# Four blocks on Trainium2: the turned row maxima of the first attention move to an edge tile's bank and three chunks later, and thirteen instead of eleven matmuls sum the NF4 planes

## What is computed

```python
# first attention, for each of the 16 batches (mask = layer norm of x, 128 x 512)
x = jnp.transpose(mask, (0, 2, 1))                  # 512 rows of 128
q, k, v = jnp.split(x @ w_in.T + b_in, 3, axis=-1)  # 8 heads of 16
scores = jnp.einsum('bqhd,bkhd->bhqk', q, k) / jnp.sqrt(d)
scores = jnp.where(jnp.abs(idx[:, None] - idx[None, :]) <= 64, scores, neg)
attn = jax.nn.softmax(scores, axis=-1)              # subtracts each row's maximum
o = jnp.einsum('bhqk,bkhd->bqhd', attn, v).reshape(n, t, e) @ w_out.T + b_out
out = jnp.einsum('nit,io->not', jax.nn.relu(transpose(o)) * encodings, w_ct) + b_ct
# NF4 round trip of the three feed-forward weights (1408 x 512 each)
idx = jnp.argmin(jnp.abs(scaled[:, None] - NF4), axis=-1)   # 16 levels
w = NF4[idx] * block_scale                                  # a scale for each 64 weights
```

## Time and profile before

| what | value |
| --- | --- |
| device time, median of 3 runs (lowest, highest) | 1466.54 us (1466.11 to 1466.81) |
| span of the profiled execution | 1463.7 us |
| TensorE matmul busy, share of that span | 1354.5 us, 93% |
| TensorE weight load busy | 813.1 us, 56% |
| VectorE busy | 1002.8 us, 69% |
| ScalarE busy | 791.5 us, 54% |
| GpSimd busy | 249.2 us, 17% |
| first attention, loop of batches | 44 to 490 us |
| of it the steady batches 2 to 13 | 119 to 433 us |

### The profile page before, as it was taken

How to read it: one execution, slowest core, us unless ns; L and a number is a source line. 1 busy time by engine, 2 the same in 40 slices (tenths; PEclk the granted TensorE clock), 3 DMA queues, 4 the chain that set the end, 5 groups by cost and what they waited for, 6 DMA issues and landing times. The chain is left out here.

```text
span 1463.7 us, 28639 instructions
## 1 busy us (share of the span) xinstructions
PE 1354.5 (93%) x8666; PEld 813.1 (56%) x8666; DVE 1002.8 (69%) x3234; ACT 791.5 (54%) x1802; POOL 249.2 (17%) x265
## 2 busy tenths in 40 slices
PE   3678999999999799999989999999789999999998
PEld 1345555555555444444455555555434777777774
DVE  8889999999997646456546788887659654545211
ACT  4777888888888733332357677776530233332331
POOL 4100000000000100000010000002411255555552
PEclk7699999999999999999999999999999999999999
DMA  8534344343440300000020000000322588888885
GB/s 261 145 87 99 91 107 106 86 119 90 107 104 17 145 1 0 0 0 0 0 75 15 16 16 14 14 1 2 146 85 93 184 247 251 255 257 246 255 233 115
DMA packets 63186, 149.52 MB, mean 102 GB/s; under 512 B 10792, under 2 KB 27830, under 8 KB 58892
## 3 DMA queue, kind: packets, MB, share of 16 engines
q1 hardware_dynamic: 49836, 115.70, 26.1%
q0 software_dynamic: 13280, 32.93, 9.6%
HBM read 113.21 MB, written 35.39 MB: 102 GB/s over the span
## 5 line engine op out<-in xcount | busy, mean ns | idle before, releaser
L776 DVE CUSTOM_DVE_ANT_0 masked_scores<-ps_max,band_mask 128x192 bf16<-128x192 f32 (+1 forms) x512 | 177.2, 383 | 20.5 <-PE ps_max L505 13.9
L383 ACT ACTIVATE probs_t<-ps_sc 128x448 f32<-128x448 f32 x256 | 138.7, 542 | 80.4 <-PE ps_sc L525 78.1
L1255 PE MATMUL f_ps<-f_xt,w_t 128*128 (+1 forms) x704 | 160.2, 382 | 2.5 <-ACT w_t L1310 2.5
L377 ACT ACTIVATE nf_above<-nf_scaled,nf_sign_at 128x512 f16<-128x512 bf16 x231 | 161.5, 715 | 0.0
L2803 DVE TENSOR_TENSOR d_inter<-d_silu_g,d_su 128x384 f32<-128x384 f32 x32 | 17.7, 554 | 159.6 <-PE d_su L2487 154.4
L1927 ACT ACTIVATE c_probs<-d_sg,c_negmax 128x128 f32<-128x128 f32 x256 | 90.3, 365 | 58.1 <-DVE c_negmax L2012 57.7
L1255 PEld LDWEIGHTS f_ps<-f_xt,w_t 128*128 128x128 bf16 x704 | 69.3, 98 | 86.7 <-issue 5.0
L2320 POOL DMA_INDIRECT out<-d_h,d_scatter_now x64 | 97.2, 1519 | 108.3 <-DMA out<-d_h,d_scatter_now 92.9
L505 PE MATMUL ps_max<-k_stack,q_stack 96*128 96x192 bf16 (+1 forms) x512 | 96.5, 272 | 19.8 <-DVE row_max L776 13.8
L2671 DVE TENSOR_SCALAR d_onehot<-d_slot_no,d_pos 128x192 bf16<-128x192 bf16 x512 | 101.0, 288 | 0.3 <-PE d_lb L2388 0.3
L505 PEld LDWEIGHTS ps_max<-k_stack,q_stack 96*128 96x128 bf16 x512 | 46.2, 101 | 92.1 <-issue 46.9
(11 more groups left out here) (381 smaller groups left out, 2830.1 us busy)
## 6 DMA issues: line engine op xcount, KB each, us to landing
d_wgu<-in_ex_gu SPq DMA_DIRECT2D x32, 1024.0 KB
d_wdown<-in_ex_d SPq DMA_DIRECT2D x32, 512.0 KB
dr_parts<-qk_parts SPq DMA_DIRECT2D x32, 384.0 KB, 4.8
q_stack<-dr_parts SPq DMA_DIRECT2D x32, 192.0 KB, 2.7
k_stack<-dr_parts SPq DMA_DIRECT2D x32, 192.0 KB, 3.3
out<-x_sb SPq DMA_DIRECT2D x21, 256.0 KB, 2.2
nf_w<-in_nf_w POOLq DMA_DIRECT2D x3, 1408.0 KB, 10.2
q_stack<-dr_parts SPq DMA_DIRECT2D x32, 128.0 KB, 2.4
```

The source lines that it names most:

```text
L377: act.activation(above[:, g, k, :], lvl[:, g, :], ACT.Sign, bias=cut[:, k - NDV:k - NDV + 1]).then_inc(s_sg, 1)
L383: act.activation(pt[:, c, :], SP[c % 2][:].rearrange("p a w -> p (a w)")[:, a:z], ACT.Exp, scale=D0 ** -0.5).then_inc(s_e, 1)
L776: op = dve.tensor_tensor_reduce(masked[:, c % 2, k, off:off + hi - lo], M[c % 2][:, k, off:off + hi - lo], mask[:, k, off:off + hi - lo], ...
L1255: mm = pe.matmul(bank[:], w12[:, m, kt, ft * P:(ft + 1) * P], xt[:, q, kt, bass.ds(g * N, N)], start=(kt == 0 and q == 0), stop=(kt == KT ...
```

## The change

Three things are changed, all in this phase.

1. The turned maxima of every unit but the very first go to `MT`, the unused 2 x 64 columns of the bank `M[1]` in chunk 3, in place of a part of `G[0]` or `G[1]`. TensorE turns them right before `smax` of chunk 3 (`MT_AT`), not after `scores` of c0 or C1's, and VectorE's `max_parts` follows the take of chunk 3, not of c1 or C2. `smax` of chunk 5, which writes all of `M[1]`, waits for `max_parts`.
2. The waits that belonged to the old places go: for `add_x` and `o_norm` before the turn, and for `max_parts` before `proj` of k and `out_proj`. `proj` of k now waits for `add_x` itself, since it writes `G[1]`; in the last batches `o_back` does.
3. VectorE folds only four of its eight planes to two (a half as wide L912), and TensorE sums 2 + 4 + 7 = 13 planes instead of 4 + 7 = 11, in two matmuls a chunk in chunks 1 to 6 and one in chunk 7.

```diff
@@ the new tile and its chunk (in phase_layer0_attention) @@
+    FIRST_MT, MT, MT_AT = G[0][0:16, 0:P], M[1][0:16, :, WIN - BAND:WIN], QT - 1
@@ TensorE @@
-            def max_t(u, g):
+            def max_t(u, g, out):
                 pe.wait_ge(s_mx, 8 * u + 8)
-                pe.transpose(G[g][0:16, 0:P], mx[:, g, :], ident[:]).then_inc(s_mT, 1)
+                pe.transpose(out, mx[:, g, :], ident[:]).then_inc(s_mT, 1)
...
-            NF_KS = [0, 2, 4, 6] + list(range(8, NLV))
-            NF_AT = [[], [0, 2], [4, 6], [8], [9, 10], [11], [12, 13], [14]]
+            NF_KS = [0, 2] + list(range(4, NLV))
+            NF_AT = [[], [0, 2], [4, 5], [6, 7], [8, 9], [10, 11], [12, 13], [14]]
...
+                    if c == MT_AT:
+                        if not final:
+                            pe.wait_ge(s_mx, 8 * (2 * i + 2) + c - 1)
+                        max_t(2 * i + 1, 1, MT)
                     if not final:
+                        if c == MT_AT + 2:
+                            pe.wait_ge(s_mp, 4 * i + 4)
                         smax(2 * i + 2, 1 - b, 0, c)
...
                     scores(2 * i, b, 0, c)
-                    if c == 0:
-                        pe.wait_ge(s_mp, 4 * i + 2)
-                        ge(pe, s_x1, i - 1)
-                        max_t(2 * i + 1, 1)
...
                     if c == 2 and not last:
-                        pe.wait_ge(s_mp, 4 * i + 4)
+                        ge(pe, s_x1, i - 1)
                         proj(i + 2, b, 1)
...
                     if not final:
+                        if c == MT_AT:
+                            pe.wait_ge(s_mx, 8 * (2 * i + 3) + c - 1)
+                            max_t(2 * i + 2, 0, MT)
+                        if c == MT_AT + 2:
+                            pe.wait_ge(s_mp, 4 * i + 6)
                         smax(2 * i + 3, 1 - b, 1, c)
...
                             pe.wait_ge(s_p1, 2 * i + 6)
                             pe.wait_ge(s_res, 2 * i + 6)
                         else:
-                            pe.wait_ge(s_mp, 4 * i + 4)
-                        if not final:
-                            if first:
-                                pe.wait_ge(s_v, 2)
-                            else:
-                                pe.wait_ge(s_on, 2 * i)
-                            if isinstance(i, int) and i == 1:
-                                nf4_mean(1, 3)
-                            max_t(2 * i + 2, 0)
+                            pe.wait_ge(s_x1, i - 1)
+                        if isinstance(i, int) and i == 1:
+                            pe.wait_ge(s_on, 2 * i)
+                            nf4_mean(1, 3)
                         pv(2 * i, b, 0, 1)
...
                     if c == 3 and not first:
-                        if not final:
-                            pe.wait_ge(s_mp, 4 * i + 6)
...
@@ VectorE @@
-            def max_parts(u, g):
-
-                mt = G[g][0:16, 0:P]
+            def max_parts(u, mt):
+
+                turned = lambda t: t.rearrange("p (a w) -> p a w", w=BAND)
...
-                dve.tensor_scalar(mparts[:, 0, :], mt, -1.0, None, ALU.mult).then_inc(s_mp, 1)
+                dve.tensor_scalar(turned(mparts[:, 0, :]), mt, -1.0, None, ALU.mult).then_inc(s_mp, 1)
...
-                    dve.tensor_tensor(above[:, g, 0:8:2, :], above[:, g, 0:8:2, :], above[:, g, 1:8:2, :], ALU.add).then_inc(s_ab, 1)
+                    dve.tensor_tensor(above[:, g, 0:4:2, :], above[:, g, 0:4:2, :], above[:, g, 1:4:2, :], ALU.add).then_inc(s_ab, 1)
...
-                    if c == 1:
-                        max_parts(2 * i + 1, 1)
+                    if c == MT_AT:
+                        max_parts(2 * i + 1, MT)
...
-                    if c == 2 and not final:
-                        max_parts(2 * i + 2, 0)
+                        if c == MT_AT:
+                            max_parts(2 * i + 2, MT)
```

More of the change, by code:

```diff
@@ L600, in _ @@
                 if g == 0:
-                    max_t(0, 0)
+                    max_t(0, 0, FIRST_MT)
             pe.wait_ge(s_mp, 2)
@@ L787, in max_parts @@
                     ge(dve, s_mw, 16 * (u - 1))
-                dve.tensor_scalar(mparts[:, 0, :], mt, -1.0, None, ALU.mult).then_inc(s_mp, 1)
+                dve.tensor_scalar(turned(mparts[:, 0, :]), mt, -1.0, None, ALU.mult).then_inc(s_mp, 1)
                 dve.wait_ge(s_mp, 2 * u + 1)
-                dve.scalar_tensor_tensor(out=mparts[:, 1, :], in0=mt, scalar=-1.0, in1=mparts[:, 0, :],
+                dve.scalar_tensor_tensor(out=turned(mparts[:, 1, :]), in0=mt, scalar=-1.0, in1=turned(mparts[:, 0, :]),
                                          op0=ALU.mult, op1=ALU.subtract).then_inc(s_mp, 1)
@@ L886, in _ @@
                 take_max(0, 0, c)
-            max_parts(0, 0)
+            max_parts(0, FIRST_MT.rearrange("p (a w) -> p a w", w=BAND))
             for c in range(8):
```

## The result

| | before | after |
| --- | --- | --- |
| median of 6 runs | 1464.97 us (1461.64 to 1466.81) | 1470.13 us (1468.13 to 1473.79) |
| ratio, 95% interval | 1 | 1.0041 (1.0025 to 1.0056) |
| span of the profiled execution | 1463.7 us | 1466.4 us |
| a steady batch, `ct` to `ct`, mean of nine | 26.13 us | 26.40 us |

The change makes the kernel 0.4% slower. Before, the nine batches take 26.07 to 26.19 us. After, they take 26.23 to 26.59, so only their mean is compared. A stretch from one `ct` to the next has the number of the batch whose `ct` ends it, counted from 0, which is one less than the `i` of `body` in which it lies: the steady batches 2 to 13 of the prediction are stretches 1 to 12 here, and the nine are 3 to 11.

The account below looks back on a forecast made before the run. TensorE and VectorE were both taken as nearly full, so the order of time set the batch. Terms of -1.2, +3.5, +0.4, +0.5 and +0.9 gave +4.1, hence 1467.8 profiled and 1470.6 us timed, range 1461 to 1476.

Parts of the forecast that it names:

- The sum: Whole kernel: first batches -1.2, twelve steady batches +3.5, last batch +0.4 and +0.5, tail +0.9; +4.1 us together.
- The step that failed: SP's stack loads behind the second `max_parts`: c0 up to 0.2 us late, hidden by the wait for `nf4_weight`.
- the third rival: The late stack, in SP's queue behind the later `max_parts`: each batch loses 0.4 us more, 1475 us; chance 0.11.
- the walk: Steady batch followed from `ct` to `ct` in the new order: 26.42 us, 0.29 more a batch; chance 0.42.
- `max_parts` ahead of `resid_part`: Chunk 3 on VectorE: `max_parts`, 0.52 us, comes ahead of `resid_part`, for which `proj_v` waits on TensorE.
- The added matmuls: Four more TensorE matmuls a batch, in c3, c5, C3 and C5: 0.215 us each, 0.86 a batch; c3's hidden.
- VectorE's saving: Half as wide fold in c4 and C4: VectorE saves 1.1 us a batch, no help from `proj_v` to c7.
- the prediction's batch 14: Batch with neither projections nor residuals, so no `proj_v` wait: 0 us, -0.5 to +0.3.
- the late read back: Last batch: last row maxima go three chunks later, their stack load is late; up to 2 us lost, 0.5 taken.
- the waits pass through: At `proj_v` in c4, TensorE stays back to back: -0.6 us a batch, 1460 us; wholly or half, chance 0.20.
- done in pieces: Turned maxima: the strided transpose runs in pieces, 0.2 us more twice a batch, 1475 us; chance 0.02.
- VectorE was the bound: VectorE's saved 1.1 us and idle 0.35 all count, fourteen batches by 1.3: 1448 us; chance 0.03.

Follow-up runs that it names:

- e3: Changed kernel with SP loading the first half's stack ahead of the write of the maxima of unit 2i+2; 1465.78 us, 1.0005 of before.
- e2: Kernel before with only the narrow fold and thirteen sums, the maxima where they were; 1469.15 us, 1.0020 of before.
- e4: Changed kernel with `resid_part` ahead of `max_parts` in chunk 3; 1470.03 us, 1.0027 of before.
- e1: Changed kernel with the old fold of eight planes and eleven sums, so the move of the maxima alone; 1474.68 us, 1.0065 of before.
- e7: e5 with the old fold of eight planes and eleven sums; 1464.66 us, 0.9988 of before.
- e5: Changed kernel with both repairs: stack ahead of the maxima write in SP's queue, `resid_part` ahead of `max_parts` in chunk 3; 1459.47 us, 0.9955 of before.
- e6: e5 with the thirteen sums in chunks 2 to 7, three in chunk 2 and none in chunk 1; 1452.92 us, 0.9905 of before.

## Why the prediction was right

The sum gave 1470.6 us and a rise of 4.1 over the profiled 1463.7. Measured were 1470.13, a rise of 5.2 between the medians, and 2.7 in the profiles. That the time was met within 0.5 us is in part luck: it was built on the median of three runs, 1466.54, and over six runs the kernel before has 1464.97, from which the same sum gives 1469.1. Point by point:

- **The batch.** Forecast 26.42, measured 26.40. Twelve stretches, 1 to 12, took 314.7 before and 318.1 after, +3.4 against the +3.5 of the sum.
- **The places.** The first sum was put at 3.44 and stands at 3.68; the others, with what was measured behind: c3 6.75 (6.98), `proj_v` 9.23 (9.48), c7 13.76 (13.96), second sum 17.59 (17.70). All are 0.1 to 0.25 late by the same cause.
- **The step that failed** is the one that looked at the loads once more. It put the second `max_parts` at 21.5, and c0 at up to 0.2 late and hidden behind `nf4_weight`. `max_parts` ended at 21.80 and c0 stood at 1.46, past the 1.3 from which the third rival was said to decide. The first sum is then at 3.68 and not 3.44, and it doesn't wait for `nf4_weight` at all, where an idle 0.4 to 0.6 had been announced. "If c0 waits for DMA and the sum of c1 for nothing else, it is the stack", the prediction said, and this is what the trace shows: from c0 to the sum of c1 the mechanism is that of the late stack, which had a chance of 0.11, and not that of the walk. The loads weren't slower than the prediction had them (3.13 for the last, against 3.2). `max_parts` was later, and the places feed each other: a late c0 makes `max_parts` later, and that the stack. A walk through a batch closes only when all its queues do, SP's too. e3 shows the price, 0.34 a batch, which is more than the whole loss.
- **What balanced it.** From the second sum to `ct` the walk had 8.83 and the trace has 8.69. The wait of `out_proj` for `max_parts` had been put at 0.05, and without it TensorE gains 0.08 ahead of `out_proj` and 0.11 in it (e2). And from c7 to the second sum it had 3.83, where 3.74 was measured: the hand-over from `nf4_weight` to the sum was put at 0.25 and is 0.15, in c1 as well (e3: the sum at 3.35, not 3.44). So the total was met with one term too small and others too large.
- **`max_parts` ahead of `resid_part`** was right in place and size: 0.52 expected, 0.53 by e4.
- **The added matmuls** of C3 and C5 were charged in full, and rightly so. Between e1 and the kernel after, which differ by them and the fold, C3 to `out_proj` goes from 0.77 to 0.99 and C5 to its `pv` from 0.92 to 1.13. That of c5 was put at 0.09 net of the wait for `v_copy`; from `proj_v` to c7 it is 4.48 after 4.44.
- **VectorE's saving** was called worthless. In the changed kernel it is not. The stretch from c3 to c7 was read as TensorE's alone. With the wide fold and `max_parts` in it VectorE has 7.09 from take to take (e1), where TensorE, by the walk and without the added matmul of c5, would have 6.8. In the change as it stands the batch is 0.33 longer without the narrow fold and its sums, of which 0.1 lies in that stretch and 0.2 in later landings of the loads. With both repairs it is 0.24 longer (e7 against e5).
- **Outside the steady batches.** The first `ct` came 1.21 sooner, as the -1.2 had it, but the traces of the other kernels have it anywhere between 114.1 and 117.8 us, so that is no evidence. Stretch 13, the prediction's batch 14, was 26.69 and is 25.22, -1.5 where I had 0 (-0.5 to +0.3): a miss, and it took back a third of what the stretches behind the first `ct` lost. In both a take in it waits some 2 us without a releaser that the profile shows, and the gain lies elsewhere in it; all seven kernels with thirteen sums have 24.8 to 25.4 there, and the two others that were tried, with eleven, 24.5 and 25.2. I haven't resolved it. Stretch 14, in the last turn of `body`, is 19.76 after 19.12, +0.64 against +0.9 expected; the sums alone make it 20.26 (e2) and the move alone 18.72 (e1), so they cost 1.14 and give 0.40. The 0.5 for the late read back hung on how long the write of the last maxima takes. In the profile after it takes 3.2 us, and a wait of 0.6 stands behind it, the last of these three lines (SP's issues, then the waits view of 455 to 470 us):

```profile
463.49 0.33 SPq L255 DMA_DIRECT2D dr_max<-max_parts  x1
466.66 0.23 SPq L259 DMA_DIRECT2D q_stack<-dr_max  x1
```

```profile
PE ps_sc L522 <- DMA q_stack<-dr_max: 0.6, 1, 0.6
```

  In e3 the same write takes 1.4 us, the wait is missing and the stretch is 19.20; it takes 1.4 to 1.8 in all eight experiments. It took 3.4 in the kernel before, without a wait behind it. So the wait of 0.6 needs both the later place and a slow write, and a slow write stands in two of the ten traces. The tail was 10.53 and is 11.39, +0.86 as worked out, and 11.39 in every kernel with thirteen sums. Together the five parts make +2.3, and the phases behind, which the change doesn't touch, +0.4.
- **The rivals.** That the waits pass through fails at the place named, `proj_v`, and holds once `resid_part` goes first and the stack is in time: e5 is 0.55 a batch below before, where the rival had 0.6. The late stack is treated above; it cost 0.34 a batch where the rival had 0.4 on top of the walk, so its 1475 was too high. The turn isn't done in pieces: its pitch is 0.11 as before. That VectorE was the bound fails: e2 saves it 1.1 a batch and is slower. Here the trace speaks against the rule of the Trainium skill that was weighed (Perfetto Trace Analysis, Identifying the Most-Contended Engine): in e6 the weight loads are busy 30.12 us of 50.35, 60%, while the matmuls leave 0.11 us free.

## What to carry to other kernels

A wait that is taken out is worth what the next wait on the same engine leaves of it: look up which semaphores the instructions right behind it need, and where the producers stand. When a step is moved, look at what stands behind it in every queue that it passes, the DMA issuer's too, and at what stands behind it on the slower engine; here two swaps of neighbouring steps turned 0.4% slower into 0.45% faster. Where two engines are both nearly full, one moves work between them last, after the order is right, since only then does the trade show its value.

## What the runs showed of the hardware

- The sixth stack load lands 5.96 us after `max_parts` before and 5.90 after (means of eight batches). Of this 0.55 passes until the first load is issued, 2.2 from the first issue to the sixth, one every 0.44, and 3.1 to 3.2 from the last issue to its landing. So loads of 64 to 192 KB are late by their issue nearly as much as by their landing.
- The place in SP's queue has a price for the write too. In steady batches the 8 KB write of the maxima takes 1.4 us from issue to landing. Behind the six loads (the second write of a batch in e3, e5, e6 and e7) it takes 2.9. That came to the surface only once each in ten batches of e3 and e7, as a wait of 0.4 and of 0.8 us of TensorE for the maxima.
- A 128x512 f32 matmul runs in two passes, each with a weight load. When a wait holds up its first weight load until the matmul itself could start, it takes some 0.1 us more: 0.96 from `out_proj` to the next instruction before, 0.86 wherever the load runs ahead.
- A PE transpose of 128x16 f32 written to two strided pieces of 64 columns had the same pitch of 0.11 us as one written in a piece.
- The write of the last row maxima took 3.4 us from issue until its read back before and 3.2 after (463.49 to 466.66), but 1.4 in six of the experiments, 1.8 in e1 and 1.7 in e7. No run tells why.
